# Four-layer residual stack on one core: quantisation in pieces of 2048 columns, and the group scales of three quarters multiplied in by ScalarE

## The chip, the cores and the metric

The kernel runs on one core of a Trainium2 chip (trn2). The metric is the device time of one execution in microseconds, lower is better; of several executions the median counts. All tensors in device memory are fp32. The engines are named as the profile names them: PE is TensorE, DVE is VectorE, ACT is ScalarE, POOL is GpSimd and SP is SyncE, which here only starts transfers.

## The reference

`x` has 64 sequences, 64 channels (rows) and 1024 columns. Four layers follow each other, each added to its input:

```python
x = x + L0(x, ...)   # long convolution per channel, causal, masked by a length
x = x + L1(x, ...)   # x @ W1.T plus gated low-rank experts (top 2 of 8)
x = x + L2(x, ...)   # x @ W2.T plus a low-rank term chosen by a label
x = x + L3(x, ...)   # x @ w_eff.T, w_eff from a quantised weight, below
```

The change lies in the making of the weight of L3. `O` and `I` are 1024, a group has 128 columns, the codebook has 64 entries:

```python
lora_delta = lora_B @ lora_A * 0.5
cb = codebook / clip(max(abs(codebook)), 1e-8)
scale = exp(scale_log)                                   # one per row and group of 128
normalized = ((weight + lora_delta).reshape(O, 8, 128)) / scale
thresholds = (cb[:-1] + cb[1:]) * 0.5
quantized = cb[searchsorted(thresholds, normalized, side='left')]
w = (quantized - normalized) + normalized
w_eff = (w * scale).reshape(O, I) + lora_delta
return x @ w_eff.T
```

## The kernel before

The program has two blocks. The first, some 367 us long, multiplies the four layers' weights into one matrix M (and low-rank parts) and makes the tables of the convolution. The second is a loop over 32 tiles of the input that applies them. The change touches the first block alone.

**The order of the first block.** The list `order` names jobs that PE works through in turn, and ACT, which takes each result out of PSUM, walks the same list. The jobs that matter here are:

- `("w2t", kt, half)`: transposes of W2, taken by ACT into `A2` (called A in the trace, line 590). POOL then adds the identity to the diagonal piece of `A2` (line 411) and counts `a2_ready`.
- `("qt", kt)`, kt from 0 to 7: the product of the weights of the layers L1 and L2, 24 matmuls each (line 530), which need `a2_ready` to be kt + 1; ACT takes them at lines 673 to 675.
- `("delta", q, n)`, four for each quarter q: the low-rank term of L3 (PE line 484), which ACT copies to `dq[q % 2]` (line 590). The four of quarter 2 stand behind `("qt", 5)`, those of quarter 3 behind `("qt", 7)`. Job results other than `qt` and `m` go to two PSUM banks in turn, so PE can be two such jobs ahead of ACT, no more (`stage_free`).
- `("a3", q, n)`: transposes of the finished quarter (line 546), which wait for `quant_done` to be q + 1.
- `("m", q, mt)`: the product with the quantised weight (line 571), taken by ACT (lines 702 and 709), with the low half made by POOL (line 450); PE may be six of them ahead. The first of a quarter waits for `a3_ready`, which POOL counts after it has added the identity (line 437).
- ACT makes the sine and exponential tables (`table`, lines 597 to 600) behind `("m", 2, 4)` and `("m", 2, 7)`, and the columns of the states (lines 607 to 616) behind `("m", 3, 0)`.

**The quantisation.** The weight of L3 is treated in four quarters of 256 rows, held as 128 partitions by 2 tiles by 1024 columns, so 2048 columns for each partition. DVE adds the low-rank term (line 897), divides by the scales (line 898), and then goes through the thresholds that are kept: line 878 makes 0 or the rise of the code, line 883 adds it to `qq[q]` ("quant" in the trace). With this codebook nine thresholds are kept. Each of the two steps is done in two pieces of 1024 columns. Lines 923 and 924 then subtract and add the normalised weight again, one tile at a time, and count `v_used`. For quarters 0 to 2 POOL finishes (`finish_quarter`): it multiplies each tile by its group scales (line 400), adds the low-rank term over the whole quarter (line 401) and counts `quant_done`. DVE finishes quarter 3 itself (lines 928 and 930). POOL calls `finish_quarter(0)` in its loop over `it`, behind the identity of `it` = 5 and ahead of those of 6 and 7, then `finish_quarter(1)`, and `finish_quarter(2)` behind the low half of `("m", 0, 4)`.

Because there are two buffers `dq`, ACT must not write the low-rank term of quarter 2 before POOL has added that of quarter 0, and likewise 3 and 1:

```python
                        if n == 0 and q >= 2:

                            act.wait_ge(quant_done, q - 1)
```

Of the kernel before, what the change touches and what calls it, by code (L numbers as in the profile page):

```python
# [23 lines left out]
F32 = mybir.dt.float32  # L24
# [3 lines left out]
ALU = mybir.AluOpType  # L28
ACT = mybir.ActivationFunctionType
AX_X = mybir.AxisListType.X  # L30

P = 128
# [7 lines left out]
def resid_stack_kernel(nc, x, lengths, languages, labels, codebook, log_dt, C_ri, log_A_real, A_imag, D_skip,  # L40
# [3 lines left out]
    NC = L // P  # L44
# [62 lines left out]
    region_q = cursor[0]  # L107
    vq = place("vq", [P, QT_TILES, L], F32)
    dq = [place(f"dq{n}", [P, QT_TILES, L], F32) for n in range(2)]
    step_t = place("step_t", [P, 2, 1024], F32)  # L110
    qq = [place(f"quant{q}", [P, QT_TILES, L], F32) for q in range(QUARTERS)]
    tau = place("tau", [P, K_CODES + 1], F32)
    cb = place("cb", [P, K_CODES], F32)
# [103 lines left out]
    with ExitStack() as ctx:  # L217
        bank = [ctx.enter_context(nc.psum_tensor(f"bank{n}", [P, BANK], F32)) for n in range(8)]

        def sem(name):  # L220
            return ctx.enter_context(nc.semaphore(name))
# [11 lines left out]
        kf_ready, kh_ready, kl_ready = sem("kf_ready"), sem("kh_ready"), sem("kl_ready")  # L233
        b3_hi, b3_lo = sem("b3_hi"), sem("b3_lo")
        quant_init, quant_done, v_used = sem("quant_init"), sem("quant_done"), sem("v_used")
        qt_full, qt_free, a3_ready = sem("qt_full"), sem("qt_free"), sem("a3_ready")
        m_full, m_taken, m_lo, lowrank_hi, lowrank_lo = sem("m_full"), sem("m_taken"), sem("m_lo"), sem("lowrank_hi"), sem("lowrank_lo")
        passed = {e: sem(f"waits_passed_{e}") for e in ("dve", "pool")}
# [63 lines left out]
        with nc.Block() as block:  # L302
# [72 lines left out]
            def _(pool):  # L375
# [18 lines left out]

                def finish_quarter(q):

                    for t in range(QT_TILES):
                        pool.wait_ge(v_used, QT_TILES * q + t + 1)
                        rounded = qq[q][:, t, :].rearrange("p (g k) -> p g k", g=NC)
                        step(pool.tensor_tensor(rounded, rounded, scale3[:, q * QT_TILES + t, :].unsqueeze(2).broadcast_to([P, NC, P]), ALU.mult))  # L400
                    pool.tensor_tensor(qq[q][:, :, :], qq[q][:, :, :], dq[q % 2][:, :, :], ALU.add).then_inc(quant_done, 1)


# [176 lines left out]
            def _(act):  # L580
# [45 lines left out]
                def init_quarter(q):  # L626

                    act.activation(qq[q][:, :, :].rearrange("p t k -> p (t k)"), cb[:, 0:1].to_broadcast([P, QCOLS]), ACT.Copy).then_inc(quant_init, 1)

                for j in order:  # L630
                    name, *which = j
                    if name == "b3t":
                        take(j, B3raw[:, which[0] * BANK:(which[0] + 1) * BANK], stage(j)[0:2 * R3, :], scale=0.5)
                        if which[0] == 1:

                            act.wait_ge(stage_free, jobno[j] + 1)
                            act.activation(B3s[:, :], B3raw[:, :], ACT.Copy).then_inc(b3_hi, 1)
                            act.wait_ge(ld_b3, 64)
                            act.activation(A3hh[:, :], A3raw[:, :], ACT.Copy).then_inc(b3_hi, 1)
                    elif name == "delta":  # L640
                        q, n = which
                        if n == 0 and q >= 2:

                            act.wait_ge(quant_done, q - 1)
                        take(j, dq[q % 2][:, n // 2, n % 2 * BANK:(n % 2 + 1) * BANK], stage(j)[:, :])
                    elif name == "w2t":
                        ot, half = which
                        take(j, A2[:, 4 * half:4 * half + 4, ot * P:(ot + 1) * P], stage(j)[:, :].rearrange("p (t k) -> p t k", t=4))
                        if j == ("w2t", 1, 1):
                            nat_sine()  # L650
                    elif name == "codesT":
                        take(j, codesT[:, :, :], stage(j)[0:K_CODES, 0:3 * P].rearrange("p (n k) -> p n k", n=3))

                        init_quarter(0)
                    elif name == "codes":
                        take(j, steps[:, :, :], stage(j)[:, 0:2 * K_CODES].rearrange("p (n k) -> p n k", n=2))
                    elif name == "nat4":
                        take(j, tabs[:, :, :], stage(j)[:, 0:4 * H].rearrange("p (q h) -> p q h", q=4))
                    elif name == "at":
                        g = which[0]  # L660
                        take(j, AT[:, 4 * g:4 * g + 4, 0:ER], stage(j)[:, :].rearrange("p (c e) -> p c e", c=4))
                    elif name == "wrt":
                        take(j, AT[:, :, ER:ER + E], stage(j)[:, 0:NC * E].rearrange("p (c e) -> p c e", c=NC))
                    elif name == "qt":
                        kt = which[0]
                        if kt == 2:

                            act.wait_ge(bw_ready, 3)
                            act.wait_ge(kpad_stored, 16)
                            act.wait_ge(early_done, 1)  # L670
                        s = 2 + 3 * (kt % 2)
                        act.wait_ge(qt_full, kt + 1)
                        act.activation(QT[:, kt, 0:BANK], bank[s][:, :], ACT.Copy)
                        act.activation(QT[:, kt, BANK:L], bank[s + 1][:, :], ACT.Copy)
                        act.activation(QT[:, kt, L:EW], bank[s + 2][:, 0:ER], ACT.Copy).then_inc(qt_free, 1)
                        if 0 < kt < QUARTERS:
                            init_quarter(kt)
                    elif name == "lap":
                        mt = which[0]
                        take(j, LAp[:, mt, :], stage(j)[:, 0:LR])  # L680
                        if mt == MT - 1:

                            act.wait_ge(stage_free, jobno[j] + 1)
                            act.activation(Mh[:, :, C_H:C_LOW], AT[:, :, :], ACT.Copy).then_inc(lowrank_hi, 1)
                            act.activation(Mh[:, :, C_LOW:MW], LAp[:, 0:NC, :], ACT.Copy).then_inc(lowrank_hi, 1)
                            act.activation(BLh[:, :], LAp[:, NC, :], ACT.Copy).then_inc(lowrank_hi, 1)
                    elif name == "a3":
                        q, n = which
                        take(j, A3[q % 2][:, 2 * n:2 * n + 2, :], stage(j)[:, :].rearrange("p (t o) -> p t o", t=2))
                    elif name == "kern":  # L690
                        g = which[0]
                        take(j, Kf[:, 16 * g:16 * g + 16, :], stage(j)[0:PARTS, :].rearrange("a (h b) -> a h b", h=16))
                        if g == 3:

                            act.wait_ge(kf_ready, 1)
                            act.activation(Kh[:, :, :], Kf[:, :, :], ACT.Copy).then_inc(kh_ready, 1)
                    else:
                        q, mt = which
                        n = mno[j]
                        rows, hi, _ = m_parts(q, mt)  # L700
                        act.wait_ge(m_full, n + 1)
                        act.activation(hi, bank[2 + n % 6][rows, 0:QO], ACT.Copy)
                        if n == 0:

                            act.wait_ge(lowrank_lo, 3)
                        if n >= 2:

                            act.wait_ge(m_lo, n - 1)
                        act.activation(m32[rows, n % 2, :], bank[2 + n % 6][rows, 0:QO], ACT.Copy).then_inc(m_taken, 1)
                        if (q, mt) in TABLES_AT:  # L710
                            table(TABLES_AT.index((q, mt)))
                        if (q, mt) == COLS_AT:
                            state_columns()

            @block.vector
            def _(dve):
# [153 lines left out]
                def rise_from(k, at, vf, qf, first):  # L870

                    k = nc.s_assert_within(k, 0, K_CODES - 1, skip_runtime_bounds_check_because="k is below n_kept")
                    assert n_ch == 2
                    for c in range(n_ch):
                        if not first:

                            dve.wait_ge(dve_step, at - 1 + c)
                        dve.tensor_scalar(step_t[:, c, :], vf[:, c * CH:(c + 1) * CH], kept_tau[:, bass.ds(k, 1)], rise[:, bass.ds(k, 1)],  # L878
                                          ALU.is_gt, ALU.mult).then_inc(dve_step, 1)
                    for c in range(n_ch):  # L880
                        cols = slice(c * CH, (c + 1) * CH)
                        dve.wait_ge(dve_step, at + c + 1)
                        dve.tensor_tensor(qf[:, cols], qf[:, cols], step_t[:, c, :], ALU.add).then_inc(dve_step, 1)  # L883
# [662 lines left out]
```

## Time and profile before

| | |
|---|---|
| time, median of 3 executions | 1117.43 us (1115.88 to 1117.84) |
| the profiled execution: its own time | 1117.58 us |
| the profiled execution: span of the core | 1115.8 us |
| mean granted clock of PE over the span | 0.979 |
| PE busy | 1028.8 us, 92% of the span |
| DVE busy | 851.0 us, 76% |
| ACT busy | 427.3 us, 38% |
| POOL busy | 286.8 us, 26% |

The own time is that of the execution that the profile was taken from; 1.8 us of it lie outside the span. Busy shares are means over a first block and a loop that have different limits, so what follows is read from the first block.

### The profile page before, as it was taken

What the parts mean: (1) busy time and instruction counts of PE and PEld (TensorE: products, weight loads), DVE (VectorE), ACT (ScalarE), POOL (GpSimd) and SP (SyncE); (2) the same over time, 40 slices, a digit from 0 to 9 for tenths busy, and PEclk for the clock granted to TensorE, in tenths of its full rate; (3) what the DMA queues carried; (4) which work ended last, traced back from release to release, by engine and by line L of the source; (5) the groups of instructions that cost most, each with busy time, mean ns of one, the idle gap of its engine ahead of it and who ended that gap; (6) DMA issues with size and microseconds to landing.
All of it is one profiled execution on the core that took longest, in us unless ns stands there. A gap on an engine that the chain in (4) does not pass through costs nothing.

```text
span 1115.8 us, 16634 instructions
## 1 busy us (share of the span) xinstructions
PE 1028.8 (92%) x4851; PEld 811.9 (73%) x4851; DVE 851.0 (76%) x1679; ACT 427.3 (38%) x851; POOL 286.8 (26%) x318
## 2 busy tenths in 40 slices
PE   3999999999979489999999999999999999999997
PEld 2545556988868378787788778877887788778785
DVE  5797988898970568877887788778877787778762
ACT  3222222222454344354434444444444444544431
POOL 1200340374342422321132113211321123112200
PEclk9999999999989689999999999999999999999999
DMA  9501010100003244534454445434543454344311
GB/s 249 146 20 57 19 38 1 38 1 1 1 1 50 36 69 87 99 69 76 81 99 73 73 81 100 76 69 82 100 79 66 85 96 83 66 85 89 71 38 38
DMA packets 317019, 74.95 MB, mean 67 GB/s; under 512 B 292979, under 2 KB 309555, under 8 KB 316987
## 3 DMA queue, kind: packets, MB, share of 16 engines
q1 hardware_dynamic: 316986, 74.56, 34.1%
q8 instruction: 15, 0.25, 0.1%
q14 instruction: 18, 0.14, 0.0%
HBM read 57.61 MB, written 16.91 MB: 67 GB/s over the span
## 4 chain that ended last, share of the span: by engine, by line
DVE 27%; issue 15%; PE 13%; ACT 9%; DVEq 1%; SPq 1%; ACTq 1%; DMA 0%
DVE ZZ L1388 7%; ACT SK L1251 5%; DVE ZZ L1379 5%; PE bank L1114 4%; DVE xT L1399 3%; PE bank L1142 3%; DVE Sl L1393 3%; PE bank L1123 2%; DVE xT L1353 2%; ACT xh L1221 2%; ACT O L1284 1%; PE bank L1169 1%; DVE low L1448 1%; PE bank L1132 1%; PE bank L1158 1%
## 5 line engine op out<-in xcount | busy, mean ns | idle before, releaser
L1068 POOL TENSOR_TENSOR Cl<-QC,Ch 128x256 fp32r<-128x256 f32 x32 | 29.7, 928 | 517.6 <-ACT Ch L1233 517.6
L1142 PE MATMUL bank<-Mh,x0l 128*128 128x512 f32 x512 | 160.9, 396 | 0.0
L1142 PE MATMUL bank<-Ml,x0h 128*128 128x512 f32 x512 | 160.5, 395 | 0.0
L1142 PE MATMUL bank<-Mh,x0h 128*128 128x512 f32 x512 | 160.3, 394 | 0.0
L1251 ACT ACTIVATE SK<-ZZ 64x448 f32<-64x448 f32 x128 | 73.8, 577 | 207.2 <-DVE ZZ L1388 204.8
L530 PE MATMUL bank<-E,A 128*128 128x512 f32 (+1 forms) x384 | 129.8, 499 | 0.0
L1388 DVE SCALAR_TENSOR_TENSOR ZZ<-ZZ,coef 128x192 f32<-128x192 f32 (+1 forms) x256 | 121.8, 516 | 10.1 <-DVE ZZ L1379 0.2
L1142 PEld LDWEIGHTS bank<-Mh,x0l 128*128 128x128 f32 x512 | 96.2, 188 | 22.9
L1142 PEld LDWEIGHTS bank<-Ml,x0h 128*128 128x128 f32 x512 | 96.2, 188 | 22.6
L530 PEld LDWEIGHTS bank<-E,A 128*128 128x128 f32 x384 | 65.6, 197 | 64.0 <-issue 64.0
L1142 PEld LDWEIGHTS bank<-Mh,x0h 128*128 128x128 f32 x512 | 94.6, 188 | 18.5
L883 DVE TENSOR_TENSOR quant<-quant,step_t 128x1024 f32<-128x1024 f32 x72 | 95.7, 1370 | 0.0
L1379 DVE SCALAR_TENSOR_TENSOR ZZ<-ZZ,coef 128x384 f32<-128x384 f32 (+1 forms) x128 | 79.9, 624 | 5.4
L878 DVE TENSOR_SCALAR step_t<-vq,steps 128x1024 f32<-128x1024 f32 x72 | 62.8, 914 | 21.1 <-DVEq L918 12.5
L1132 PE MATMUL bank<-Ml,x0h 128*128 128x296 f32 x256 | 76.8, 300 | 0.0
L1132 PE MATMUL bank<-Mh,x0h 128*128 128x296 f32 x256 | 76.4, 299 | 0.0
L1132 PE MATMUL bank<-Mh,x0l 128*128 128x296 f32 x256 | 76.4, 299 | 0.0
L571 PE MATMUL bank<-A3b,QT 128*128 128x256 f32 x288 | 65.4, 388 | 7.2 <-issue 7.2
L1264 ACT ACTIVATE x0h<-xT 128x512 fp32r<-128x512 f32 x64 | 40.2, 632 | 81.0 <-DVE xT L1399 81.0
L1242 ACT ACTIVATE ZZ<-bank 64x448 f32<-64x448 f32 x128 | 68.6, 536 | 2.7 <-PE bank L1103 0.4
L1428 DVE TENSOR_SCALAR gsm<-gsm 128x1 f32<-128x1 f32 x32 | 4.9, 154 | 82.3 <-ACT gsm L1268 82.3
L571 PEld LDWEIGHTS bank<-A3b,QT 128*128 128x128 f32 x288 | 55.8, 195 | 15.5 <-issue 7.6
(283 smaller groups left out, 2022.9 us busy)
## 6 DMA issues: line engine op xcount, KB each, us to landing
X<-in_x SPq DMA_DIRECT2D x256, 64.0 KB, 2.4
XT<-in_x SPq DMA_DIRECT2D x256, 64.0 KB, 2.3
out_x<-O SPq DMA_DIRECT2D x64, 256.0 KB, 3.2
toep<-kpad SPq DMA_DIRECT2D x128, 64.0 KB, 2.2
E<-in_L_cond_W SPq DMA_DIRECT2D x8, 512.0 KB, 6.7
W2s<-in_L_cond_W SPq DMA_DIRECT2D x8, 512.0 KB, 4.3
vq<-in_L_cond_weight SPq DMA_DIRECT2D x8, 512.0 KB, 3.4
LA<-in_L_cond_lora_A SPq DMA_DIRECT2D x8, 80.0 KB, 3.4
```

Of the source, the lines that this page charges most:

```text
L530: last = pe.matmul(bank[s + n][:, 0:b - a], A2[:, it, kt * P:(kt + 1) * P], E1[:, it, a:b], start=(it == 0), stop=(it == NC - 1))
L571: last = pe.matmul(bank[2 + n % 6][0:rows, 0:QO], lhs, A3[q % 2][:, kt, :], start=(kt == 0), stop=(kt == NC - 1))
L878: dve.tensor_scalar(step_t[:, c, :], vf[:, c * CH:(c + 1) * CH], kept_tau[:, bass.ds(k, 1)], rise[:, bass.ds(k, 1)], ALU.is_gt, ALU.mult). ...
L883: dve.tensor_tensor(qf[:, cols], qf[:, cols], step_t[:, c, :], ALU.add).then_inc(dve_step, 1)
L1114: last = pe.matmul(psY[hh][:, :].rearrange("p (c b) -> p c b", b=B), toep[:, hh, w, :], (xh, xl)[p][:, :, hh * B:(hh + 1) * B], start=(n = ...
L1132: last = pe.matmul(psL[:, 0:LOWC], xs[:, c, :], ms[:, c, L:MW], start=(c == 0 and n == 0), stop=False, skip_group_check=True)
L1142: pe.matmul(psO[nh][:, :], xs[:, c, :], ms[:, c, nh * BANK:(nh + 1) * BANK], start=(c == 0 and n == 0), stop=False)
L1242: act.activation(ZZ[hh * N:(hh + 1) * N, :, ri, :], psZ[hh][ri * N:(ri + 1) * N, 0:SB].rearrange("p (c b) -> p c b", b=B), ACT.Copy).then_ ...
L1251: act.activation(SK[ri * N:(ri + 1) * N, hh, :].rearrange("p (c b) -> p c b", b=B), ZZ[hh * N:(hh + 1) * N, :, ri, :], ACT.Copy).then_inc( ...
L1264: act.activation(x0h[:, :, cols], xT[:, :, cols], ACT.Copy).then_inc(x0h_done, 1)
L1379: dve.scalar_tensor_tensor(ZZ[:, dst, :, :], ZZ[:, src, :, :], coef[:, bass.ds(i, 1), power, 0], ZZ[:, dst, :, :], ALU.mult, ALU.add).then ...
L1388: dve.scalar_tensor_tensor(ZZ[:, dst, to, :], ZZ[:, src, of, :], coef[:, bass.ds(i, 1), power, n], ZZ[:, dst, to, :], ALU.mult, ALU.add).t ...
```

## The change

Two things are changed. The thresholds are gone through in one piece of 2048 columns for each step in place of two of 1024. And the multiplication by the group scales of quarters 0, 1 and 2 is taken from POOL (two instructions of 1024 columns for each quarter) and given to ACT, as sixteen instructions of 128 columns for each quarter, each with its scale read from a column of `scale3`. POOL keeps the addition of the low-rank term, and waits for ACT's count `rescaled`. Quarter 3 stays with DVE.

```diff
-    step_t = place("step_t", [P, 2, 1024], F32)
+    step_t = place("step_t", [P, 1, QCOLS], F32)
...
                 def finish_quarter(q):
 
-                    for t in range(QT_TILES):
-                        pool.wait_ge(v_used, QT_TILES * q + t + 1)
-                        rounded = qq[q][:, t, :].rearrange("p (g k) -> p g k", g=NC)
-                        step(pool.tensor_tensor(rounded, rounded, scale3[:, q * QT_TILES + t, :].unsqueeze(2).broadcast_to([P, NC, P]), ALU.mult))
+                    pool.wait_ge(rescaled, QT_TILES * (q + 1))
                     pool.tensor_tensor(qq[q][:, :, :], qq[q][:, :, :], dq[q % 2][:, :, :], ALU.add).then_inc(quant_done, 1)
...
+                def rescale_quarter(q):
+
+                    for t in range(QT_TILES):
+                        act.wait_ge(v_used, QT_TILES * q + t + 1)
+                        for g in range(NC):
+                            group = qq[q][:, t, g * P:(g + 1) * P]
+                            last = act.activation(group, group, ACT.Copy, scale=scale3[:, q * QT_TILES + t, g:g + 1])
+                        last.then_inc(rescaled, 1)
...
                         if 0 < kt < QUARTERS:
                             init_quarter(kt)
+                        if kt == 5:
+                            rescale_quarter(0)
+                        if kt == NC - 1:
+                            rescale_quarter(1)
...
+                        if (q, mt) == (0, 4):
+                            rescale_quarter(2)
...
-                    assert n_ch == 2
+                    assert n_ch == 1
                     for c in range(n_ch):
                         if not first:
 
-                            dve.wait_ge(dve_step, at - 1 + c)
+                            dve.wait_ge(dve_step, at - n_ch + 1 + c)
```

The names in the listings below are those of the program (quant_70 is `qq[0]`, dq_67 is `dq[0]`, A_85 is `A2`), and the line numbers are each kernel's own. First ACT, from the job `("w2t", 6, 0)` to the taking of the low-rank term of quarter 2; before:

```order
L590 ACTIVATE A_85<-bank 128x4x128 [waits stage_full] x2
L673 ACTIVATE QT<-bank 128x512 [waits qt_full]
L674 ACTIVATE QT<-bank 128x512
L675 ACTIVATE QT<-bank 128x128
L590 ACTIVATE dq_67<-bank 128x512 [waits stage_full,quant_done]
L590 ACTIVATE dq_67<-bank 128x512 [waits stage_full] x3
L590 ACTIVATE A_85<-bank 128x4x128 [waits stage_full] x2
```

And the same place of ACT in the changed kernel:

```order
L588 ACTIVATE A_85<-bank 128x4x128 [waits stage_full] x2
L680 ACTIVATE QT<-bank 128x512 [waits qt_full]
L681 ACTIVATE QT<-bank 128x512
L682 ACTIVATE QT<-bank 128x128
L634 ACTIVATE quant_70<-quant_70,scale_82 128x128 [waits v_used]
L634 ACTIVATE quant_70<-quant_70,scale_82 128x128 x7
L634 ACTIVATE quant_70<-quant_70,scale_82 128x128 [waits v_used]
L634 ACTIVATE quant_70<-quant_70,scale_82 128x128 x7
L588 ACTIVATE dq_67<-bank 128x512 [waits stage_full,quant_done]
L588 ACTIVATE dq_67<-bank 128x512 [waits stage_full] x3
L588 ACTIVATE A_85<-bank 128x4x128 [waits stage_full] x2
```

The sixteen multiplications of quarter 0 now stand between the taking of `("qt", 5)` and the taking of the low-rank term of quarter 2. Those of quarter 1 stand in the same way behind `("qt", 7)`. Next POOL in its loop over `it` and behind it, before:

```order
L411 TENSOR_TENSOR A_85<-A_85,ident 128x128 [waits stage_free] x4
L400 TENSOR_TENSOR quant_70<-quant_70,scale_82 128x1024 [waits v_used]
L400 TENSOR_TENSOR quant_70<-quant_70,scale_82 128x1024 [waits v_used,pool_step]
L401 TENSOR_TENSOR quant_70<-quant_70,dq_67 128x2048 [waits pool_step]
L411 TENSOR_TENSOR A_85<-A_85,ident 128x128 [waits stage_free] x2
```

The same place of POOL in the changed kernel:

```order
L409 TENSOR_TENSOR A_85<-A_85,ident 128x128 [waits stage_free] x4
L399 TENSOR_TENSOR quant_70<-quant_70,dq_67 128x2048 [waits rescaled]
L409 TENSOR_TENSOR A_85<-A_85,ident 128x128 [waits stage_free] x2
L399 TENSOR_TENSOR quant_71<-quant_71,dq_68 128x2048 [waits rescaled]
```

Here the addition now waits for ACT, and the identities of `it` = 6 and 7 stand behind it.

## Rows read from the trace of the kernel before

**Rows 1.** Who PE waited for, 94 to 366 us: total, times, longest us.

```profile
PE bank L571 <- issue: 7.2, 1, 7.2
PE bank L484 <- ACT dq L590: 0.6, 2, 0.3
```

**Rows 2.** PE in time: start us, us, instructions, idle time before and its releaser.

```profile
127.35 1.04 PE L489 MATMUL bank<-ident,W2s 128*128 128x128 f32 x8
128.22 15.68 PE L530 MATMUL bank<-E,A 128*128 128x512 f32 x48
...
145.74 0.51 PE L484 MATMUL bank<-A3hh,B3s 128*128 128x512 f32 x1 [0.32 <-ACT dq L590]
...
147.45 1.87 PE L489 MATMUL bank<-ident,W2s 128*128 128x128 f32 x8
149.12 32.25 PE L530 MATMUL bank<-E,A 128*128 128x512 f32 x96
...
291.17 0.60 PE L546 MATMUL bank<-ident,quant 128*128 128x128 f32 x4
...
324.47 16.15 PE L571 MATMUL bank<-A3b,QT 128*128 128x256 f32 x64 [7.21 <-issue]
```

**Rows 3.** ACT in time where it takes quarter 2's and quarter 3's low-rank term.

```profile
145.07 1.11 ACT L590 ACTIVATE dq<-bank 128x512 f32<-128x512 f32 x2
...
182.54 1.10 ACT L590 ACTIVATE dq<-bank 128x512 f32<-128x512 f32 x2
```

**Rows 4.** ACT and PE in time around the low-rank term of quarter 1.

```profile
88.42 1.92 ACT L628 ACTIVATE quant<-cb 128x2048 f32<-128x2048 f32 x1
...
90.88 0.51 PE L484 MATMUL bank<-A3hh,B3s 128*128 128x512 f32 x1 [2.19 <-ACT dq L590]
```

**Rows 5.** POOL and DVE in time while POOL finishes quarters 0 and 1.

```profile
115.96 4.20 POOL L400 TENSOR_TENSOR quant<-quant,scale 128x1024 f32<-128x1024 f32 x2
120.23 4.84 POOL L401 TENSOR_TENSOR quant<-quant,dq 128x2048 f32<-128x2048 f32 x1
120.62 5.53 DVE L883 TENSOR_TENSOR quant<-quant,step_t 128x1024 f32<-128x1024 f32 x1
...
162.49 4.51 POOL L401 TENSOR_TENSOR quant<-quant,dq 128x2048 f32<-128x2048 f32 x1
```

**Rows 6.** Groups of ACT by form: busy us, mean ns of one.

```profile
L624 ACT ACTIVATE nat<-nat,half_pi 64x64 f32<-64x64 f32 x1 | 0.3, 348 | 0.0
L686 ACT ACTIVATE BLh<-LAp 128x160 fp32r<-128x160 f32 x1 | 0.3, 322 | 0.0
L623 ACT ACTIVATE nat<-nat 64x64 f32<-64x64 f32 x1 | 0.3, 256 | 0.0
```

**Rows 7.** ACT in time, two copies from SBUF with no wait between them.

```profile
208.77 1.11 ACT L684 ACTIVATE Mh<-AT 128x1088 fp32r<-128x1088 f32 x1
209.79 1.26 ACT L685 ACTIVATE Mh<-LAp 128x1280 fp32r<-128x1280 f32 x1
```

**Rows 8.** DVE in time: one threshold, a whole quarter's multiplication, quarter 3's end, tables.

```profile
52.05 2.29 DVE L898 TENSOR_TENSOR vq<-vq,inv_scale 128x2048 f32<-128x2048 f32 x1
...
56.23 1.53 DVE L878 TENSOR_SCALAR step_t<-vq,steps 128x1024 f32<-128x1024 f32 x2 [1.89 <-DVEq L918]
57.68 2.35 DVE L883 TENSOR_TENSOR quant<-quant,step_t 128x1024 f32<-128x1024 f32 x2
...
285.74 2.70 DVE L930 TENSOR_TENSOR quant<-quant,dq 128x2048 f32<-128x2048 f32 x1
...
307.88 1.97 DVE L746 SCALAR_TENSOR_TENSOR rem<-turns,rem 128x1344 f32<-128x1344 f32 x1
```

**Rows 9.** ACT in time, the start of the second table.

```profile
310.63 1.28 ACT L597 ACT_TABLE_LOAD   x1
```

**Rows 10.** PE in two stretches: length, busy us (instructions), granted clock, DMA.

```profile
147.90:151.90 4.00, 4.00 (x11) 0.58 0.00 0
...
321.05:328.40 7.35, 3.93 (x9) 0.56 0.01 2
```

More of the change, by code:

```diff
@@ L235, in resid_stack_kernel @@
         quant_init, quant_done, v_used = sem("quant_init"), sem("quant_done"), sem("v_used")
+        rescaled = sem("rescaled")
         qt_full, qt_free, a3_ready = sem("qt_full"), sem("qt_free"), sem("a3_ready")
```

## The prediction

> **What bounds the kernel now.** I read the waits of PE first, because the busy shares name PE as the fullest engine. From 94 us to the end of the first block PE waits for three things only [rows 1]: twice 0.3 us for ACT to take the low-rank term, and once 7.2 us ahead of the product with quarter 3. The reader is to see that there is no wait for the quantisation in that list. So in this stretch PE's queue sets the end, and a step on another engine counts only if PE comes to wait for it. PE in order of time shows how late each could be. The transposes of quarter 3 start at 291.17 [rows 2], and DVE has that quarter ready at 285.74 + 2.70 = 288.44 [rows 8], 2.7 us ahead. That is the tightest of the four quarters.
>
> The 7.2 us wait is ACT's. DVE hands over the second reduced angle at 307.88 + 1.97 = 309.85 [rows 8], and ACT starts the table at 310.63 with no idle time before it [rows 9]. ACT came there by walking the list behind PE, so a later PE moves this wait along and does not shrink it. The loop of tiles behind the first block does not know when it was started. A delay of PE in the first block is a delay of the end.
>
> **The change, part by part.**
>
> *One piece in place of two.* A threshold costs DVE 1.53 us for two comparisons and 2.35 for two additions [rows 8]. One addition of 2048 columns should take about the 2.29 of line 898 [rows 8]; one comparison should take somewhat under 1.53, as one fixed part is saved. Against that, each instruction must now end before the next starts, where before the pieces overlapped. I take zero, with bounds of 0.2 us less and 0.6 more for each of the 36 thresholds, that is 7 us less to 22 more on DVE. Neither end reaches PE: the part below makes PE ask for quarter 3 some 20 us later, on top of the 2.7 there are, and the multiplications gone from POOL free DVE, which stood for most of POOL's work (one addition of 1024 columns took 5.53 us beside POOL's addition, where two usually take 2.35 [rows 5, 8]). Price on the end: 0. If that cover were gone, every microsecond of DVE beyond the 2.7 would count.
>
> *The multiplications on ACT.* No row has a scale read from a column. A copy of 128x160 from SBUF takes 0.322 us [rows 6] and one of 128x1280 takes 1.26 [rows 7], 0.84 ns for each further column, so one of 128 takes 0.295. A column as operand adds about 0.09, by the two forms of 64x64 with and without `half_pi` [rows 6]. Two such copies in a row overlap by 0.1 (one starts at 208.77 and takes 1.11, the next starts at 209.79 [rows 7]). So 0.39 - 0.10 = 0.29 for each, and sixteen with the last tail come to 4.8 us. Bounds: with no price for the column 3.2 us; with no overlap 6.2 us. The Trainium skill's page "ScalarE: Activation LUTs", section "What ACT_TABLE_LOAD costs", prices each operand of this kind at 93 ns and the overlap at 93 ns; by it sixteen would come to 4.8 us as well, and no run here shows such an operand as a scale.
>
> *Where they stand.* This is what I take to decide the case. Those of quarter 0 stand on ACT between the taking of `("qt", 5)` and that of the low-rank term of quarter 2, and the latter also waits for `quant_done`, that is for POOL's addition to quarter 0. Before, POOL had ended that addition at 120.23 + 4.84 = 125.07 [rows 5], 20 us before ACT came at 145.07 [rows 3], and the wait cost nothing. Now the addition cannot start until ACT has scaled both tiles, which ACT only does at 145. ACT then stands through POOL's whole addition. Queued behind ACT's wait are the four low-rank results, and PE, which has only two banks for them: it already waited there [rows 2], so there is no slack. A smaller case of the same can be seen one quarter earlier. ACT's filling of `qq[2]`, 1.92 us at 88.42, stands in the same place, and PE waits 2.19 there [rows 4] in place of 0.32 [rows 2]: PE pays for all of it.
>
> The addition costs 4.51 us when POOL finds DVE idle and 4.84 when it doesn't [rows 5]. POOL and DVE exclude each other, and DVE's longest piece is now 2.29 us, so POOL can wait for that long before it gets in. DVE is inside the thresholds at both places. I take 4.5 + 0.9 = 5.4 us, with bounds of 4.5 and 6.8. Hand-overs between engines add 0.1. So one place costs 4.8 + 5.4 + 0.1 = 10.3 us.
>
> The same happens again behind `("qt", 7)`. The taking of quarter 3's low-rank term, at 182.54 before [rows 3], waits for the addition to quarter 1, which had ended at 162.49 + 4.51 = 167.00 [rows 5] and now waits for ACT at 182.5. Two places: 20.6 us. The identities of `it` = 6 and 7 that stand behind POOL's addition are late too, but PE needs the first only after quarter 2's low-rank term, so it hides under the same wait.
>
> *The third quarter.* Its multiplications stand behind `("m", 0, 4)`. There PE may be six results of 16 matmuls ahead. Sixteen take 16.15 / 4 = 4.0 us where the clock is partly low [rows 2], so not under 2.0 at the full one, and six are worth 12 us or more, against the 4.8 for which ACT is held. POOL has two multiplications less to do, and the transposes of quarter 2 come much later. I take 0.
>
> *The clock.* After a stretch in which PE works little, the granted clock goes to the lower of its levels, 1.2 GHz. Behind the low-rank term of quarter 2 it was 0.58 over 4 us [rows 10], and the work there was stretched by (1.87 - 1.04) + (32.25 - 2 x 15.68) = 1.7 us [rows 2]. Behind the 7.2 us wait it was again low, 0.56 from 321.05 to 328.40 [rows 10], with 3.93 us of work in it, which at half speed costs 2.0. Each of the two places thus pays the low clock already, and I add 0.4 for each: 0.8, bounds 0 and 2.
>
> *Sum.* 20.6 + 0.8 = 21.4 us. On the profiled execution's 1117.58 this is 1139.0. Its time lies 0.15 above the median of the runs, so for a median 1138.8 us.
>
> **The rivals.**
>
> *Only ACT's own work counts* (POOL's addition is somehow over in time): 2 x 4.9 + 0.8 = 10.6, so 1128.0 us. For it speaks that the wait cost nothing before [rows 3, 5]. Against it: the addition needs both tiles of ACT's product. 0.04.
>
> *A later wait takes up part of it.* If the 7.2 us wait were DVE's and not ACT's, PE would arrive later and wait less: 1138.8 - 7.2 = 1131.6 us. DVE is only 0.8 us ahead of ACT there [rows 8, 9], which is what speaks for it. 0.03.
>
> *DVE sets the end, and is freed.* POOL's multiplications took 4.20 us for two and DVE stood meanwhile. If DVE's chain through quarter 3 and the tables carried the 7.2 us wait, freeing DVE would end it: 1117.4 - 7.2 = 1110.2 us. It decides only if DVE is late for the table at 310.63, and it is 0.8 early [rows 8, 9]; and PE's two stalls would have to be absent. 0.02. The Trainium skill's "GPSIMD Engine Reference", section "1. Specifications", says that POOL shares its SBUF interfaces with DVE instructions that have two SBUF inputs. The trace agrees (5.53 us for one addition [rows 5]), and by that rule taking work off POOL speeds DVE up.
>
> *Dearer instructions.* ACT at 6.2, POOL at 6.8 and the clock at its bound: 2 x 13.1 + 2.0 = 28.2, so 1145.6 us. The same side holds a DVE that loses over 0.6 us for each threshold. 0.05.
>
> **How the numbers follow.** The forecast has 0.86. Its own bounds are 2 x (3.2 + 4.5 + 0.1) = 15.6, so 1133.0 us, and the 28.2 of above. Both costs at their upper end at both places is unlikely, so I stop at 1144. The range 1133.0 to 1144 leaves out both cases below it and the last one. What a measurement of this kernel can tell from no change is 0.2%, some 2 us. Faster by more than that has the 0.02 of the freed DVE, within it 0.01, slower 0.97.
>
> **What would show it.** In the profile after: ACT waits about 5 us for POOL's addition before the low-rank terms of quarters 2 and 3; PE waits about 10 us for ACT at the third matmul group of each; sixteen copies start some 0.29 us apart; the 7.2 us wait is still there, near 345 us; the waits of PE hold nothing for the quantised quarters. The prediction is wrong if ACT does not wait for `quant_done`, if PE's wait in either place is well under 8 us, or if the 7.2 us wait has shrunk.

## The result, and the profile after

The changed kernel takes 1138.09 us (median of 4, 1136.11 to 1139.39), the kernel before beside it 1116.66 us (median of 4). The ratio is 1.019 with a 95% interval of 1.0169 to 1.021: 21 us slower. The forecast was 1138.8 us, with a range of 1133.0 to 1144.0.

Who PE waited for in the changed kernel, from 94 to 390 us (total, times, longest us), to be held against [rows 1]. The last row lies behind the end of the first block, and the kernel before has the same one there:

```profile
PE bank L482 <- ACT dq L588: 19.4, 2, 9.7
PE bank L569 <- issue: 7.2, 1, 7.2
PE bank L1105 <- POOL QB L1061: 4.0, 1, 4.0
```

The wait for ACT's taking of the low-rank term has grown from 0.6 to 19.4 us, still two times. The 7.2 us ahead of the product with quarter 3 is unchanged, and nothing in the list is a wait for a quantised quarter. ACT in order of time, with both places (start us, us, instructions, idle time and its releaser), against [rows 3]:

```profile
143.34 4.78 ACT L634 ACTIVATE quant<-quant,scale 128x128 f32<-128x128 f32 x16
152.72 1.08 ACT L588 ACTIVATE dq<-bank 128x512 f32<-128x512 f32 x2 [4.60 <-POOL quant L399]
...
191.10 4.78 ACT L634 ACTIVATE quant<-quant,scale 128x128 f32<-128x128 f32 x16
200.48 1.08 ACT L588 ACTIVATE dq<-bank 128x512 f32<-128x512 f32 x2 [4.60 <-POOL quant L399]
```

POOL in order of time, against [rows 5]:

```profile
148.19 4.49 POOL L399 TENSOR_TENSOR quant<-quant,dq 128x2048 f32<-128x2048 f32 x1 [33.87 <-ACT quant L634]
...
195.95 4.49 POOL L399 TENSOR_TENSOR quant<-quant,dq 128x2048 f32<-128x2048 f32 x1 [36.16 <-ACT quant L634]
```

And PE, against [rows 2]:

```profile
153.37 0.80 PE L482 MATMUL bank<-A3hh,B3s 128*128 128x512 f32 x1 [9.68 <-ACT dq L588]
...
156.26 1.97 PE L487 MATMUL bank<-ident,W2s 128*128 128x128 f32 x8
158.02 31.92 PE L528 MATMUL bank<-E,A 128*128 128x512 f32 x96
...
201.13 0.79 PE L482 MATMUL bank<-A3hh,B3s 128*128 128x512 f32 x1 [9.67 <-ACT dq L588]
...
343.58 15.83 PE L569 MATMUL bank<-A3b,QT 128*128 128x256 f32 x64 [7.21 <-issue]
...
380.54 3.62 PE L569 MATMUL bank<-A3b,Bw 128*96 128x256 f32 x16
```

The reader can follow one place from end to end. ACT scales from 143.34 to 148.12, POOL starts its addition 0.07 us later and ends at 152.68, ACT takes the first low-rank result at 152.72, and PE, which stood since 143.7, goes on at 153.37. POOL itself had stood for 33.87 us: the work was given to ACT at a time long after the data was ready. DVE was done with quarter 3 at 276.7 in place of 288.4 (1.7 us of that is an earlier start of this execution), with no use made of it. Both parts of the change help DVE there: with the scaling alone (e2 below) it was done at 281.2, with one piece alone (e1) at 285.3.

### The profile page after: what moved, and what is told of

Its sections match the earlier page's. It is cut to its first block, busy times and chain, and to the rows that moved or that the text cites. A ratio compares the mean times of both kernels' runs of the same rounds, so it can differ in the third digit from the quotient of the medians.

```text
span 1135.4 us, 16553 instructions
## 1 busy us (share of the span) xinstructions
PE 1030.7 (91%) x4851; PEld 814.1 (72%) x4851; DVE 835.2 (74%) x1607; ACT 440.8 (39%) x899; POOL 272.0 (24%) x312
## 4 chain that ended last, share of the span: by engine, by line
DVE 26%; issue 15%; PE 13%; ACT 9%; DVEq 1%; SPq 1%; ACTq 1%; DMA 0%
DVE ZZ L1401 7%; ACT SK L1264 5%; DVE ZZ L1392 4%; PE bank L1127 4%; DVE xT L1412 3%; PE bank L1155 3%; DVE Sl L1406 3%; PE bank L1136 2%; DVE xT L1366 2%; ACT xh L1234 2%; ACT O L1297 1%; PE bank L1182 1%; DVE low L1461 1%; PE bank L1145 1%; PE bank L1171 1%
## 5 line engine op out<-in xcount | busy, mean ns | idle before, releaser
L896 DVE TENSOR_TENSOR quant<-quant,step_t 128x2048 f32<-128x2048 f32 x36 | 90.3, 2509 | 1.2
L891 DVE TENSOR_SCALAR step_t<-vq,steps 128x2048 f32<-128x2048 f32 x36 | 53.9, 1498 | 24.1 <-DVE quant L896 12.1
L1355 DVE STREAM_TRANSPOSE xq<-X 128x512 f32<-128x512 f32 x64 | 45.1, 707 | 28.0 <-PEq L303 17.7
```

The costliest lines, as they stand in the source:

```text
L1355: dve.transpose(xq[:, :, hh * B:(hh + 1) * B].rearrange("p c (h b) -> p h c b", h=HB), X[:, :, hh * NC:(hh + 1) * NC, ::-1]).then_inc(xq_d ...
```

## The experiments

Theory P, that of the prediction: the loss comes from where the scaling stands in ACT's queue, with POOL's addition behind it. Its rivals are D (DVE's one-piece steps) and W (the work moved, wherever it stands). Ratios are to the kernel before on the same chip.

**e1_one_piece.** The kernel before with only this:

```diff
-    step_t = place("step_t", [P, 2, 1024], F32)
+    step_t = place("step_t", [P, 1, QCOLS], F32)
...
-                    assert n_ch == 2
+                    assert n_ch == 1
...
-                            dve.wait_ge(dve_step, at - 1 + c)
+                            dve.wait_ge(dve_step, at - n_ch + 1 + c)
```

> The kernel before with one piece of 2048 columns for each threshold step and nothing else. Theory P (the place of the scaling on ScalarE and the addition behind it make the loss): no change, within 2 us of the kernel before, since VectorE has 2.7 us of slack ahead of the transposes of quarter 3 and the one-piece steps cost it about as much. Rival D (VectorE's steps make the loss): slower by a large part of the 20 us.

Measured 1119.38 us, ratio 1.0029 (1.002 to 1.0037). Rival D falls, for this is 3 us and not 20. But 3 us are not nothing, and theory P had given them no price. The waits of PE in this run, 94 to 390 us, show one that the kernel before has not:

```profile
PE bank L571 <- ACT A3b L590: 1.3, 1, 1.3
```

DVE isn't late in this run (quarter 3 is ready at 285.3). POOL is, where it finishes quarter 2 while DVE goes through the thresholds of quarter 3; POOL and ACT in order of time:

```profile
231.34 6.45 POOL L401 TENSOR_TENSOR quant<-quant,dq 128x2048 f32<-128x2048 f32 x1
237.74 3.90 POOL L437 TENSOR_TENSOR A3b<-A3b,ident 128x128 f32<-128x128 f32 x2
```

```profile
242.35 0.39 ACT L709 ACTIVATE m<-bank 128x256 f32<-128x256 f32 x1 [5.62 <-POOL Ml L450]
...
244.31 0.59 ACT L590 ACTIVATE A3b<-bank 128x512 f32<-128x512 f32 x1
```

In the kernel before POOL took 4.86 us for the addition and 2.83 us for the identities, ACT waited 2.89 us for POOL, and this piece of A3b was taken at 242.07, 2.2 us earlier, in an execution that reached this place 1 us later. This is theory C, tested below: the longer pieces of DVE keep POOL out for longer.

**e2_scaling_only.** The changed kernel with the lines of e1 turned back, so the scaling on ACT alone.

> The changed kernel with the thresholds in two pieces of 1024 again, so the scaling on ScalarE alone. Theory P: all of the loss, 19 to 22 us slower than the kernel before, with two waits of TensorE of about 9.7 us. Rival D: much less than that.

Measured 1137.78 us, ratio 1.0193 (1.0178 to 1.0208). All of the loss is in the scaling. The two waits are 10.4 and 9.7 us; at the first of them POOL's addition took 5.20 us.

**e3_scaling_earlier.** The changed kernel with two numbers changed:

```diff
-                        if kt == 5:
+                        if kt == 4:
                             rescale_quarter(0)
-                        if kt == NC - 1:
+                        if kt == NC - 2:
                             rescale_quarter(1)
```

> The changed kernel with the scaling of quarter 0 moved from behind qt 5 to behind qt 4, and that of quarter 1 from behind qt 7 to behind qt 6; the same instructions, one product earlier. Theory P: ScalarE scales and GpSimd adds while TensorE is in the 16 us product that follows, both waits fall back to 0.3 us, and the time is that of the kernel before, within 2 us. Rival W (the amount of work moved, or its contention, makes the loss, wherever it stands): still 15 us or more slower.

Measured 1116.45 us, ratio 1.0 (0.9992 to 1.0009). The same instructions, one product earlier, and the 21 us are gone. ACT in order of time:

```profile
128.77 4.78 ACT L634 ACTIVATE quant<-quant,scale 128x128 f32<-128x128 f32 x16
...
145.16 1.11 ACT L588 ACTIVATE dq<-bank 128x512 f32<-128x512 f32 x2
...
166.94 4.78 ACT L634 ACTIVATE quant<-quant,scale 128x128 f32<-128x128 f32 x16
...
182.46 1.11 ACT L588 ACTIVATE dq<-bank 128x512 f32<-128x512 f32 x2
```

The scaling costs the same 4.78 us, but now PE is in a product of 16 us meanwhile. The two transposes of W2 that ACT takes late behind the first place sit in PE's two banks and hold nobody, and the low-rank term waits for nobody either. That POOL's first addition took 6.57 us here did no harm. Rival W falls.

**e4_scalar_work_only.** The kernel before, with sixteen copies of the same kind on ACT ahead of line 675:

```diff
+                        if kt in (5, NC - 1):
+                            for n in range(2 * NC):
+                                again = QT[:, kt - 3 + n // NC, n % NC * P:(n % NC + 1) * P]
+                                act.activation(again, again, ACT.Copy, scale=iota[:, 1:2])
                         act.activation(QT[:, kt, L:EW], bank[s + 2][:, 0:ER], ACT.Copy).then_inc(qt_free, 1)
```

> The kernel before, with sixteen copies of 128 columns on ScalarE, scale read from a column that holds 1.0, added behind the products qt 5 and qt 7 (in place, on finished parts of QT); GpSimd keeps its multiplications and additions as before. Theory P with two parts: ScalarE's own work costs 4.7 us at each place plus some clock, so 10 to 12 us slower, and TensorE waits about 5.0 us at each place. If GpSimd's addition did not matter, this run would be as slow as the changed kernel, 20 us.

Measured 1128.16 us, ratio 1.0116 (1.01 to 1.0131), two waits of PE of 5.0 us. ACT's own work, with what the clock adds behind it, is a little over half of the loss: 12.0 of 21 us. The two waits grew by 9.3 us in all. The work of PE right behind them (to the end of the products and transposes) was stretched by another 1.6 and 1.9 us, and the 64 matmuls behind the 7.2 us wait by 0.3.

**e5_pool_add_twice.** The changed kernel with one step more in `finish_quarter`:

```diff
                     pool.wait_ge(rescaled, QT_TILES * (q + 1))
+                    if q < 2:
+                        step(pool.tensor_tensor(qq[q][:, :, :], qq[q][:, :, :], dq[q % 2][:, :, :], ALU.add))
```

> The changed kernel with GpSimd's addition of the low-rank term made twice for quarters 0 and 1 (so the term is in the result twice there). Theory P: ScalarE stands through the addition, so each further one of 4.5 us comes to the end in full, 9 to 10 us slower than the changed kernel, some 30 us above the kernel before, with two waits of TensorE of about 14.2 us. If the addition were hidden, this run would be as fast as the changed kernel.

Measured 1150.06 us, ratio 1.0292 (1.0277 to 1.0307), 12 us above the changed kernel where 9 to 10 were expected. The waits of PE are 15.1 us each, 5.4 more than in the changed kernel. POOL's steps explain these 10.8 us:

```profile
148.59 5.34 POOL L400 TENSOR_TENSOR quant<-quant,dq 128x2048 f32<-128x2048 f32 x1 [34.17 <-ACT quant L636]
154.01 4.49 POOL L401 TENSOR_TENSOR quant<-quant,dq 128x2048 f32<-128x2048 f32 x1
```

At each place one addition took 4.49 us and the other 5.3. Every microsecond of POOL there comes to the end. What is left of the difference is not in the two waits: PE's work right behind each of them was 0.8 us longer than in the changed kernel, and a wait of 0.4 us for ACT's A3b came ahead of the product with quarter 1.

**e6_earlier_and_tables.** e3 with ACT's tables two products earlier, to use what DVE has gained:

```diff
-        TABLES_AT = [(2, 4), (2, 7)]
+        TABLES_AT = [(2, 2), (2, 5)]
```

> The kernel with the scaling one product earlier (e3_scaling_earlier), and the two tables of ScalarE behind m(2,2) and m(2,5) in place of m(2,4) and m(2,7). VectorE hands over the second reduced angle near 300.6 us there, ahead of m(2,5) near 303. Theory T (the 7.2 us wait of TensorE is ScalarE's second table standing ahead of the last transposed piece of quarter 3): the wait falls to under 2 us, and the time is 7 to 9 us below the kernel before, 1107 to 1110 us. Rival (VectorE or GpSimd ends that wait): no change.

Measured 1111.01 us, ratio 0.9955 (0.9941 to 0.9969), 5 us faster than the kernel before. The direction is right and the size short of the 7 to 9 expected, since the wait fell to 2.8 us and not under 2. What PE waits for last is POOL, which adds the identities; here POOL, and then PE:

```profile
313.65 2.03 POOL L448 TENSOR_TENSOR R1l<-m,R1h 128x256 fp32r<-128x256 f32 x1
315.65 2.36 POOL L435 TENSOR_TENSOR A3b<-A3b,ident 128x128 f32<-128x128 f32 x2
```

```profile
318.11 14.05 PE L569 MATMUL bank<-A3b,QT 128*128 128x256 f32 x64 [2.75 <-issue]
```

That last step was POOL's in the kernel before too. ACT's table ended there at 318.67, POOL had stood for ACT, and PE started at 324.47, 0.1 us behind POOL:

```profile
319.30 1.62 POOL L450 TENSOR_TENSOR R1l<-m,R1h 128x256 fp32r<-128x256 f32 x1 [6.86 <-ACT m L709]
320.88 3.49 POOL L437 TENSOR_TENSOR A3b<-A3b,ident 128x128 f32<-128x128 f32 x2
```

So the 7.2 us wait is ACT's table and 5.1 us of POOL behind it, and the earlier table takes 4.5 us away. The 64 matmuls behind the wait take 14.05 us in place of the 16.15 of [rows 2]. With the shorter wait the granted clock does not fall: it is 1.00 from 318 to 322 us, where before it was 0.50 in the 4 us behind the wait.

**e7_before_tables.** The kernel before with the same line of `TABLES_AT`.

> The kernel before with only the two tables moved to m(2,2) and m(2,5). VectorE hands over the angles at 299.4 and 309.85 us, so ScalarE would wait for both, and the second table would still end near 318. Expected within 2 us of the kernel before: the earlier place needs the time that VectorE gains where GpSimd has no multiplications. If this run gains 7 us too, the scaling on ScalarE is not needed for it.

Measured 1119.07 us, ratio 1.0014 (1.0006 to 1.0023). The wait is still there, at 7.3 us, and ACT's wait of 8.0 us for DVE ahead of the first table gives PE a new one of 1.3 us. But the second table did not end near 318, as I had expected:

```profile
314.60 1.32 ACT L600 ACTIVATE expo<-expo 128x1344 f32<-128x1344 f32 x1
```

```profile
316.55 3.62 POOL L450 TENSOR_TENSOR Ml<-m,Mh 128x256 fp32r<-128x256 f32 x2 [5.47 <-ACT m L709]
320.12 2.04 POOL L450 TENSOR_TENSOR R1l<-m,R1h 128x256 fp32r<-128x256 f32 x1
322.12 2.35 POOL L437 TENSOR_TENSOR A3b<-A3b,ident 128x128 f32<-128x128 f32 x2
```

It ended at 315.92, 2.8 us earlier than in the kernel before, and nothing was gained: a table that stands further ahead in ACT's queue has more of POOL's work behind it, here 7.9 us from 316.55 to 324.47 where it was 5.1. In e6 the same steps of POOL took 8.0 us, but the table ended at 309.42. So the tables can be moved with profit only where DVE is early enough. Scaling on ACT is what makes it so: e8 below differs from this run in the scaling alone and has the gain.

**e8_tables_two_pieces.** e6 with two pieces again.

> As e6_earlier_and_tables, with the thresholds in two pieces of 1024 again. The one-piece run was 3.2 us slower than the kernel before, with GpSimd's addition to quarter 2 stretched from 4.86 to 6.45 us and a wait of TensorE of 1.3 us ahead of the product with quarter 1; e3_scaling_earlier has 0.7 us of that wait. With two pieces that wait should go: 0 to 3 us faster than e6_earlier_and_tables.

Measured 1110.48 us, ratio 0.9941 (0.9928 to 0.9954). The interval overlaps that of e6, so this run alone does not tell the two apart. Neither of the two has the 0.7 us wait of e3, so two pieces had nothing to win.

**e9_earlier_two_pieces.** e3 with two pieces again.

> The kernel with the scaling one product earlier (e3_scaling_earlier), thresholds in two pieces of 1024, tables where they were. e3 had a wait of 0.7 us for the transposed pieces of quarter 2 and was as fast as the kernel before. Theory C (the longer pieces of VectorE keep GpSimd out, and GpSimd's lateness reaches TensorE through ScalarE): no such wait, 0 to 2 us faster than the kernel before.

Measured 1116.14 us, ratio 1.0002 (0.9994 to 1.0011). The 0.7 us wait of e3 is gone, as expected, but the time isn't told apart from that of e3.

**e10_two_pieces_in_q3 and e11_one_piece_in_q3.** The kernel before, with `n_ch` chosen for each quarter:

```diff
...
+                    n_ch = 1 if q < QUARTERS - 1 else 2
+                    CH, per = QCOLS // n_ch, 2 * n_ch
```

That is e10; in e11 the first line has `==` in place of `<`.

> The kernel before with one piece for each threshold step in quarters 0, 1 and 2 and two pieces in quarter 3. GpSimd finishes quarter 2 while VectorE is in quarter 3. Theory C: its addition takes 4.9 us again and the time is that of the kernel before, within 1.5 us. Rival (the one-piece steps cost by themselves, in every quarter): some three quarters of the 3.2 us of e1_one_piece, 2 us or more.

> The counterpart: one piece for each threshold step in quarter 3 alone. Theory C: the wait of 1.3 us ahead of the product with quarter 1 is there, and the time is 2 to 4 us above the kernel before, as in e1_one_piece. Rival: under 1 us.

e10: 1116.8 us, ratio 1.0002 (0.9992 to 1.0012). e11: 1119.03 us, ratio 1.0041 (1.0024 to 1.0059). One piece in three quarters costs nothing, one piece in the fourth costs all that e1 cost. POOL's addition to quarter 2 in e10, and then in e11, where the wait is 1.8 us:

```profile
233.93 5.38 POOL L401 TENSOR_TENSOR quant<-quant,dq 128x2048 f32<-128x2048 f32 x1
```

```profile
231.50 6.44 POOL L401 TENSOR_TENSOR quant<-quant,dq 128x2048 f32<-128x2048 f32 x1
237.91 3.90 POOL L437 TENSOR_TENSOR A3b<-A3b,ident 128x128 f32<-128x128 f32 x2
```

```profile
PE bank L571 <- ACT A3b L590: 1.8, 1, 1.8
```

Theory C stands. By the medians the cost is 3.3 us in e1 and 2.5 in e11, whose ratio is pulled up by three executions of 1125 to 1126 us. In the profiled executions PE's work from the third low-rank matmul of quarter 2 to the end of the first block is 2.4 us longer in e1 and 2.5 in e11 than in the kernel before, and 0.2 shorter in e10. Of the 2.4 and 2.5 us the wait is 1.3 and 1.8. Nearly all the rest is the 64 matmuls behind the 7.2 us wait, which took 17.06 us in e1 and 16.76 in e11 in place of 16.15.

**e12_tables_earliest.** e8 with the tables behind m(2,1) and m(2,4).

> As e8_tables_two_pieces, with the tables behind m(2,1) and m(2,4). The 2.8 us wait that is left there ends with GpSimd's identities, which were slow beside VectorE's steps on the second table (R1l 2.03 and two identities 2.36 us). One product earlier VectorE should be done sooner and GpSimd quick: the wait falls to 0 to 1.5 us, and the time to 1107 to 1110 us.

Measured 1109.65 us, ratio 0.9943 (0.993 to 0.9956). The wait fell to 1.4 us as expected, and the median lies just inside the 1107 to 1110, but the interval is that of e8. ACT now waits 3.4 us for DVE ahead of the first table, so DVE has nothing left to give there. e8 and e12 are the fastest versions tried, some 6.5 us below the kernel before.

## Why the prediction was right, point by point

**What bounds the kernel.** Right. PE's queue sets the end of the first block: e4 and e5 put 4.6 and 5.4 us more of waiting on PE at each place, 9.3 and 10.8 us in all, and the end moved by 12 us each time, by the waits and by what the clock added to them.

**The multiplications on ACT.** Forecast 4.8 us for sixteen, measured 4.78, and 4.77 with another column as scale in e4. The price of a column, which no row of before had, was right.

**The wait behind them.** Right in its mechanism: ACT waits 4.60 us for POOL at each place, and PE 9.7. The size of POOL's part was 0.9 us too high. I had 5.4 for an addition that may have to wait until DVE lets it in. At the first place POOL came just between two short steps of DVE, at the second in the gap of a loop, and took 4.49 both times, which is luck of the moment: e2 (5.20) and e5 (5.34, 4.49) show that POOL's wait for DVE exists and depends on it. The wait of PE grew by 9.36 us at each place, where 10.3 were forecast.

**The clock.** Mis-sized: 0.8 us was forecast for both places together, and 2.1 us came. From the third low-rank matmul to the transposes of W2 it took 1.71 us before (145.74 to 147.45 [rows 2]) and 2.89 now. The granted clock of PE in the stretch from the end of the wait to the next product, in the changed kernel (length, busy, clock, DMA) at each place:

```profile
153.37:158.02 4.65, 4.65 (x12) 0.50 0.32 113
201.13:207.72 6.59, 6.46 (x21) 0.54 0.03 4
```

Before, the clock fell only when the low-rank matmuls were over (0.58 from 147.9 on [rows 10]). Now it has fallen during the wait, and the work starts at 1.2 GHz. From the third low-rank matmul to the end of the products and transposes behind it the two places are longer by 0.9 and 1.2 us, 2.1 in all, just over the upper bound of 2. The same two stretches are longer than before by 3.5 us in e4, 1.9 in e2 and 3.7 in e5, with waits of 5.0, about 10 and 15.1 us, so this cost does not follow the length of the wait. What sets it was not tested.

**The sum.** In the profiled executions, from the third low-rank matmul's normal place to the end of PE's work in the block: 2 x 9.36 of waits, 2.1 of clock, and 0.3 less behind the 7.2 us wait, 20.5 us where 21.4 were forecast. The two errors, 1.9 too much for waits and 1.3 too little for the clock, stood against each other; that the sum came within 1 us is luck to that extent. The spans differ by 19.6 because the profiled execution of the changed kernel reached the place 1.7 us earlier and its loop took 0.8 us longer; over all runs that place lies between 143.2 and 146.2 us, and the loop takes 749.8 to 752.1 us. In the chances, slower adds up to 0.98 and not 0.97; no rival stands for the 0.01 of no change.

**The later wait.** Right: 7.21 before and 7.21 after. But "The 7.2 us wait is ACT's" is only a part of it. Against e3, e6 moves the tables alone, and the wait falls to 2.8: 4.5 us of it are the table's. PE starts 0.1 us behind POOL's identities in both kernels, and in e7 a table that ended 2.8 us earlier left the wait as it was, because POOL had more to do behind it. The forecast does not depend on this, since both move along with a later PE.

**The third quarter.** Right in the changed kernel; there is no wait there.

**One piece.** The step that failed is "Price on the end: 0. If that cover were gone, every microsecond of DVE beyond the 2.7 would count". In the changed kernel the price was indeed nothing. But the reason was wrong, and alone the edit costs 3 us: what suffers is not DVE's own end but POOL, which it keeps out, and from there ACT and PE. I had counted POOL's burden on DVE and not DVE's on POOL. The zero for DVE's own work was near: from start to start two undisturbed thresholds took 8.3 us in two pieces and 8.4 in one.

**The rivals.** "Only ACT's own work counts" (1128.0 us) fell. e4 is nearly that kernel, at 1128.16 us, but the agreement is luck: the rival adds 10.6 us, e4 was 12.0 above a kernel before that took 1116.12 us beside it, with 9.3 us of waits and more of the clock than the 0.8 of the sum. "A later wait takes up part of it" fell with the 7.21. "DVE sets the end, and is freed": DVE was freed, by 10 us at the end of quarter 3 counted from the same place of PE, and did not set the end; e6 and e8 turn this into 5 to 6.5 us, but only with the tables moved.

## What to carry to other kernels

When work is moved to another engine, ask where in that engine's queue it will stand, and what stands behind it. A queue with 60% of idle time is still full at the moment when the bounding engine wants its result taken. A short wait already seen at that place (here 0.3 us, and 2.2 behind a filling of 1.9) says that there is no slack, and one product earlier there was plenty.

A semaphore wait that costs nothing is a link all the same. Here POOL's addition ended 20 us ahead of ACT's wait, and 15.5 the second time, and one moved step turned it into 4.6 us, twice.

What an engine off the bounding path gains is worth something only if the step that waits for it is moved up too. And before such a step is moved, ask which engine has the last step ahead of the wait: here ACT's table could end 2.8 us earlier for nothing (e7), because POOL's steps behind it grew by as much.

## What the runs showed of the hardware that I had not expected

POOL's addition of 128x2048 took 4.49 to 4.53 us when it found DVE between two steps. When one of DVE's was in flight it took the rest of that step and 4.3 to 4.4 us more: with 0.47 us left 4.84 us (the kernel before), with 0.86 left 5.25 (quarter 2 of the changed kernel), with 2.07 left 6.45 (e1), with 2.20 left 6.57 (e3).

So longer pieces on DVE are not free for POOL, but the moment counts as much. Beside the thresholds of quarter 3 it took 6.44 and 6.45 us with pieces of 2048 columns where it came early in one (e11, e1), 5.10 and 4.52 where it did not (e3, e6), and 4.86 and 5.38 with pieces of 1024 (before, e10). Once it took 6.25 us with pieces of 1024 (e12, quarter 1): two of DVE's additions stood one behind the other, and it got in only after both.

ACT's copies of 128x128 with a scale from a column took 387 to 413 ns each, but sixteen in a row took 4.78 us, 0.3 us for each: they overlap.
